# Scores in single precision on 32 by 64 tiles, values on 64-column tiles, a 64-row mask, the transposed context kept in memory, and new orders in both layers

## The reference, cut to what matters

```
x = x + tanh(g0) * attention0(norm(x), c)      # 16 heads of 8; mask in chunks of 32 keys
x = x + tanh(f0) * expert(norm(x))             # 8 experts 128->512->128, one for each token
x = x + tanh(g1) * attention1(norm(x), c)      # 16 heads of 8; causal mask and padding mask
x = x + tanh(f1) * mixture(norm(x))            # 16 experts: q, k, v of each token are sums over
                                               # experts, one head of 128, outputs again a sum
attention: softmax((xn Wq + bq)(c Wk + bk)^T / sqrt(8) + mask) (c Wv + bv) Wo + bo
```

## Time and profile before

| | |
|---|---|
| median of 3 runs | 1886.92 us (1884.77 to 1887.55) |
| profiled execution | 1886.17 us |
| its span | 1884.5 us, 51137 instructions |
| TensorE, matmul busy | 1728.3 us, 92% |
| VectorE / ScalarE / GpSimd busy | 1382.6 (73%) / 1132.2 (60%) / 1184.9 us (63%) |
| TensorE's granted clock over the span | 0.967 |
| first layer, experts, second layer | to about 428, 455 to 621, from there to the end |
| load of a slot, issue to landing | 2.1 us |

### The profile page before, as it was taken

The page is one execution under the profiler, slowest core; times in us unless marked ns, Lnnn a source line. Parts: engine busy times, 40 slices in busy tenths (PEclk is TensorE's granted clock), DMA queues, the critical chain, the costliest instruction groups (busy, mean ns, idle before and its releaser), DMA issues.

```text
span 1884.5 us, 51137 instructions
## 1 busy us (share of the span) xinstructions
PE 1728.3 (92%) x16279; PEld 1504.1 (80%) x16280; DVE 1382.6 (73%) x3767; ACT 1132.2 (60%) x2854; POOL 1184.9 (63%) x1682
## 2 busy tenths in 40 slices
PE   5999999983988589999999999999999999999986
PEld 4788888863888468888888888888888888888875
DVE  3676667654444247898888888898887888898875
ACT  3777777752544345666666666666666666666543
POOL 2444444444344347777877777787778777777764
PEclk8999999996999789999999999999999999999998
DMA  2311222233443100000000000000000000000000
GB/s 64 107 65 66 67 67 67 67 97 92 122 125 100 45 22 14 18 15 26 15 18 21 21 15 19 19 22 18 15 25 17 18 15 27 16 15 15 7 4 9
DMA packets 92898, 75.41 MB, mean 40 GB/s; under 512 B 13328, under 2 KB 80176, under 8 KB 92592
## 3 DMA queue, kind: packets, MB, share of 16 engines
q1 hardware_dynamic: 84992, 58.96, 10.4%
q0 software_dynamic: 5120, 12.62, 2.2%
q10 hardware_dynamic: 2608, 1.59, 0.4%
HBM read 36.91 MB, written 19.44 MB: 30 GB/s over the span
## 4 chain that ended last, share of the span: by engine, by line
PE 60%; DVE 7%; issue 5%; POOL 2%; SPq 1%; ACT 1%; DMA 1%; POOLq 0%; DVEq 0%; ACTq 0%
PE s_bank L1724 12%; PE s_bank L1726 10%; PE s_bank L1725 10%; PE po L1553 3%; PE tb L1538 3%; PE s_bank L1518 3%; PE s_bank L1666 2%; PE po L1678 2%; DVE qkv L1319 2%; PE s_bank L1855 2%; PE m L1803 1%; PE s_bank L1864 1%; DVE lg L1246 1%; PE tb L1724 1%; PE po L1724 1%
## 5 line engine op out<-in xcount | busy, mean ns | idle before, releaser
L694 POOL TENSOR_TENSOR qkv<-qkv,scaled 128x384 f32<-128x384 f32 x480 | 491.3, 1024 | 169.8 <-ACT scaled L907 130.7
L907 ACT ACTIVATE scaled<-s_bank,wg 128x384 f32<-128x384 f32 x448 | 252.9, 582 | 187.0 <-PE s_bank L1726 182.9
L1319 DVE SCALAR_TENSOR_TENSOR qkv<-s_bank,wg,qkv 128x384 f32<-128x384 f32 x448 | 274.6, 613 | 119.4 <-PE s_bank L1726 105.9
L1724 PE MATMUL s_bank<-proj_hi,hn_hi 128*128 128x384 f32 x896 | 340.0, 379 | 19.2 <-DVE qkv L1319 18.4
L1725 PE MATMUL s_bank<-proj_lo,hn_hi 128*128 128x384 f32 x896 | 302.7, 338 | 0.0
L1726 PE MATMUL s_bank<-proj_hi,hn_lo 128*128 128x384 f32 x896 | 302.4, 337 | 0.0
L793 ACT ACTIVATE pT<-tb 128x512 f32<-128x512 f32 x256 | 152.3, 595 | 75.9 <-PE tb L1538 75.4
L1724 PEld LDWEIGHTS s_bank<-proj_hi,hn_hi 128*128 128x128 f32 x896 | 169.6, 189 | 34.7 <-DVE qkv L1319 28.3
L1553 PEld LDWEIGHTS po<-vb,pT 128*64 128x64 f32 x4096 | 145.5, 137 | 62.3 <-issue 62.3
L1553 PE MATMUL po<-vb,pT 128*64 128x18 f32 x4096 | 170.9, 214 | 5.5 <-ACT pT L793 5.5
L1725 PEld LDWEIGHTS s_bank<-proj_lo,hn_hi 128*128 128x128 f32 x896 | 170.5, 190 | 0.8
(11 more groups left out here) (287 smaller groups left out, 4228.2 us busy)
## 6 DMA issues: line engine op xcount, KB each, us to landing
kx<-k SPq DMA_DIRECT2D x256, 64.0 KB
xs<-sorted_in SPq DMA_DIRECT2D x72, 128.5 KB, 2.1
cin<-in_ctx SPq DMA_DIRECT2D x64, 128.0 KB, 2.1
sorted_out<-yo SPq DMA_DIRECT2D x72, 64.0 KB, 1.8
xin<-in_x SPq DMA_DIRECT2D x32, 128.0 KB, 2.2
w<-in_L_ffn_W SPq DMA_DIRECT2D x16, 256.0 KB, 3.9
out_x<-res SPq DMA_DIRECT2D x32, 128.0 KB
sorted_in<-zrow ACTq DMA_DIRECT2D x1, 1156.5 KB, 6.5
```

Source lines behind the costliest of these rows:

```text
L694: g.tensor_tensor(into, into, scaled[m % SCALED][:, 0:cols], ALU.add).then_inc(dense_added, 1)
L907: ins = act.activation(into, bank[:, 0:3 * D], ACT.Copy, scale=wg[v % 4][:, 1, k:k + 1])
L1319: v.scalar_tensor_tensor(out=acc, in0=bank[:, 0:3 * D], scalar=wg[w % 4][:, 0, k:k + 1], in1=acc, op0=ALU.mult, op1=ALU.add).then_inc(dens ...
L1724: pe.matmul(bank[:, 0:cols], hi[:, tile], of(proj_hi), start=True, stop=False)
```

## The change

It has six parts. (a) Queries and keys are stored once, in full precision (`qT`, `kT`, `kx`), and the scores are 16 products on tiles of 32 rows by 64 columns; the corrections on VectorE are gone. (b) The masks follow: 8 products in both layers; in the second one half of the heads' mask stands on rows 0 to 63 and the other on 64 to 127. (c) Values are 8 products on 64-column tiles, a layout that puts even heads on partitions 0 to 63 and odd heads on 64 to 127. (d) The first layer's transposed context is stored to a buffer `ctx_cols` and loaded in the second, which transposes only the tokens. (e) The padding mask is loaded once as 128 by 64, transposed by TensorE and kept with keys on the partitions; its constants are built at body 0 of the first layer; the first norm is applied by GpSimd in the first layer (`apply_norm` there). (f) VectorE sums the outputs with small multiply-adds as they come, and all five engines have new orders.

The diff, cut to its core; allocations, semaphore names and waits that follow from these edits are left out.

```diff
 def place_keys(layer, v):
-        sp.dma_start(kx[r:P:4, r, :, :].bitcast(F32), k2[r:P:4, :, :].bitcast(F32)) ...
+        sp.dma_start(kx[r:P:4, r, :], kT[r:P:4, :]).then_inc(q["keys_placed"], 16)
+def store_context(v, par):
+    sp.wait_ge(s[0]["xcT_ready"], v + 1)
+    sp.dma_start(ctx_cols[bass.ds(v * P, P), :], xcT[par][:, 1, :]).then_inc(ctx_stored[par], 16)
 def body0(u, par):        # Sync
+        store_context(u + 2, par)
         place_keys(0, u + 2)
-            sp.wait_ge(setup["consts"], 5)
 def load_context(v):
-    sp.wait_ge(s[1]["xc_in_psum"], v - 1)
-    sp.dma_start(cin[par][:, :, :], tokens(a["ctx_1024"], v)) ...
+    sp.wait_ge(s[1]["qk_in_psum"], v - 1)
+    sp.wait_ge(s[1]["v_in_psum"], v - 1)
+    sp.dma_start(xcT[par][:, 1, :], ctx_cols[P * v:P * v + P, :]) ...
 def upper_consts():       # GpSimd, now called in body 0 of the first layer
-    g.tensor_copy(pad_u8[rows, :, :], pad_all[rows, :, h, :]) ...
 def pad_row(v):           # GpSimd: 3 steps on 128 columns become 2 on 256
+    step(g.tensor_tensor(pad_unit, bcast(not_causal, 4, 1), bcast(pad_keys[:, 4 * v:4 * v + 4], LEN, 2), ALU.mult))
+    g.tensor_tensor(mask_keys[v % 2], pad_unit, bcast(causal, 4, 1), ALU.add)
+def apply_norm(v, par):   # GpSimd, first layer, behind norm(0, v); ScalarE's is gone there
+        ins = g.tensor_scalar(xn[:, t, :], xin[par][:, t, :], rstd[:, t:t + 1], shift[:, 1, t:t + 1], ALU.mult, ALU.add)
 def body1(u):             # GpSimd
-    ... add(u, "q", 8, 9, 10); lower_heads(u - 1); add(u, "q", 11, 12, 13, 14, 15) ...
+    ... add(u, "q", 8, 9); lower_heads(u - 1); add(u, "q", 10); lower_hidden(u + 1); add(u, "q", 11, 12, 13, 14, 15) ...
 def keys(layer, v):       # ScalarE; queries(layer, v) is a second function like it
-    act.activation(k2[:, 0, :], m1[:, 256:512], ACT.Identity, bias=...)
+    act.activation(kT[:, :], m1[:, 256:512], ACT.Identity, bias=...).then_inc(q["k_ready"], 1)
-def lower_k(layer, w):    # VectorE, and lower_q
 def take_part(u, kind, k):   # VectorE, kind "o"
-    v.tensor_tensor(outs[:, 4 * k:4 * k + 4, :], bank, bcast(wg[w % 4][:, 0, 4 * k:4 * k + 4], D, 2), ALU.mult)
+    for e in range(4 * k, 4 * k + 4):
+        into, cols = halves[:, 0, e % 2, :], slice(D * (e % 4), D * (e % 4) + D)
+        if e < 2:
+            ins = v.tensor_scalar(into, bank[:, cols], wg[w % 4][:, 0, e:e + 1], None, ALU.mult)
+        else:
+            v.wait_ge(f["row_sums"], E1 * w + e - 1)
+            ins = v.scalar_tensor_tensor(out=into, in0=bank[:, cols], scalar=wg[w % 4][:, 0, e:e + 1],
+                                         in1=into, op0=ALU.mult, op1=ALU.add)
+        ins.then_inc(f["row_sums"], 1)
+    v.wait_ge(f["row_sums"], E1 * w + 4 * k + 4)
+    v.sem_inc(dense_used[0], 1)
-def fold, total_rows      # total_groups and total are half as wide
+def head_values(q, layer, par):   # TensorE, in values and upper_values
+    by_head = wv[layer][:, :].rearrange("c (r h d) -> c h r d", h=2, d=HD)
+    for seq in range(4):
+        for h in range(2):
+            ins = pe.matmul(m0[64 * h:64 * h + 64, LEN * seq:LEN * seq + LEN],
+                            xcT[par][:, 1, LEN * seq:LEN * seq + LEN], by_head[:, h, :, :], ...)
 def scores(layer, v, par):
-        pe.matmul(s_bank[j][:, :], early_rows[quad, :, :], late_keys[quad, :, :], ...)
+        for half in range(2):
+            pe.matmul(s_bank[j][64 * half:64 * half + 64, :], early_rows[quad, half, :], late_keys[quad, :, :], ...)
 def head_products(q, v):
-            for qs, ks in ((0, 0), (0, 1), (1, 0)):
-                for j in range(QUADS):
-                    ins = pe.matmul(s_bank[j][:, UNIT * t:UNIT * t + UNIT], beside[:, at:at + 2, :], kx[quad, :, ks, own], ...)
+            for j in range(QUADS):
+                quad = slice(32 * j, 32 * j + 32)
+                ins = pe.matmul(s_bank[j][64 * half:64 * half + 64, UNIT * t:UNIT * t + UNIT],
+                                qT[quad, own], kx[quad, :, own], ...)
 def upper_scores(u):
-    for j in range(QUADS):
-        pe.matmul(s_bank[j][:, :], identb[:, :], bcast(mask_pad[v % 2][:, :, :], 4, 2), ...)
+    for t in range(2):
+        mask = mask_keys[v % 2][:, 2 * t:2 * t + 2, :].rearrange("p h q -> p (h q)")
+        for j in (0, 2, 1, 3):
+            keys = slice(LEN * (j // 2), LEN * (j // 2) + LEN)
+            pe.matmul(s_bank[j][:, UNIT * t:UNIT * t + UNIT], mask[keys, :], bcast(identb[keys, keys], 4, 1), ...)
 def upper_in(v):
-    for t in range(2):
-        ins = pe.transpose(m0[:, P * (2 + t):P * (3 + t)], cin[v % 2][:, t, :], ident[:, :])
```

More of the change, by code:

```diff
@@ L233, in flamingo @@
             yo = [sb_first(f"yo{b}", [P, D]) for b in range(2)]
-        x3 = [sb(f"x3{b}", [P, 2, D]) for b in range(4)]
+        x3 = [sb(f"x3{b}", [P, 2, D]) for b in range(5)]
         hn = sb("hn", [P, 2, D])
@@ L530, in upper_consts @@
             def upper_consts():
-                for par in range(2):
-                    g.wait_ge(scattered[par], 16 * UNITS)
-                g.wait_ge(load["pad"], 16)
-                for h in range(2):
-                    rows = slice(LEN * h, LEN * h + LEN)
-                    g.tensor_copy(pad_u8[rows, :, :], pad_all[rows, :, h, :]).then_inc(setup["consts"], 1)
-                    g.wait_ge(setup["consts"], 4 + h)
-                for t, v in ((causal[:, :, :], 0.0), (not_causal[:, :, :], MASKED)):
+                for t, v in ((causal[:, :], 0.0), (not_causal[:, :], MASKED)):
                     done.free(g.memset(t, v))
@@ L1346, in total_groups @@
+                        v.wait_ge(f["row_sums"], E1 * w + 4 * k + 4)
+                        v.sem_inc(dense_used[0], 1)
             def total_groups(w):
                 if exists(w):
-                    step = Steps(v, f["sum_steps"], w, SUM)
-                    step.n = 3
                     v.wait_ge(dense_added, added_no(w + 1, "o", 3) + 1)
-                    step.wait()
-                    step.free(v.tensor_tensor(sums[:, :, 0:2, :], sums[:, :, 0:2, :], sums[:, :, 2:4, :], ALU.add))
+                    v.tensor_tensor(halves[:, 1, :, :], sums[:, 0:2, :], sums[:, 2:4, :], ALU.add)\
+                        .then_inc(f["sum_steps"], 1)
@@ L1354, in total @@
             def total(w):
                 if exists(w):
-                    step = Steps(v, f["sum_steps"], w, SUM)
-                    step.n = 4
-                    step.wait()
-                    step.free(v.tensor_tensor(oall[:, :, :], sums[:, :, 0, :], sums[:, :, 1, :], ALU.add))
-                    step.end()
+                    v.wait_ge(f["row_sums"], E1 * w + E1)
+                    v.wait_ge(f["sum_steps"], 2 * w + 1)
+                    v.tensor_tensor(oall[:, :, :], halves[:, :, 0, :], halves[:, :, 1, :], ALU.add)\
+                        .then_inc(f["sum_steps"], 1)
```

474 lines of the change are left out of this document (237 added, 237 removed).

## The result

The kernel after takes 1731.77 us (median of 4, 1726.85 to 1733.89), the kernel before 1887.24 beside it (4 runs): ratio 0.9174, 95% interval 0.915 to 0.920. The profiled execution has a span of 1732.2 us against 1884.5.

The account below looks back on a forecast made before the run. TensorE's list per unit was taken to bound both layers: 32 x 1.5 = 48, 32 x 0.95 = 30, and 9.5 between the layers make 88 us, so 1886 - 88 = 1798 us, range 1750 to 1860.

Parts of the forecast that it names:

- Part 1: Scores, both layers: 16 products on 32x64 tiles take 1.15 us instead of 1.63, 0.48 less per unit.
- rivals 1 and 4: Scores: rival 1 (0.10); or a product's second pass holds up all behind it, 1945 us, slower (0.06).
- rival 1: Column halves sharing row groups don't overlap: scores 1.8 us, values and masks without gain, 1858 us; chance 0.10.
- Part 2: Masks: 8 products on half tiles save 0.3 us per unit in the second layer, 0 in the first.
- Part 3: Values: 8 products 64 by 64 instead of 0.81 us, 0.3 less per unit in both layers.
- Part 4: Fewer changes of tile form at 0.2 us a trip: 0.6 less per second-layer unit, 0.4 in the first.
- Part 5: Context no longer transposed in the second layer: 0.2 us less per unit, later key transfers hidden.
- Part 6: Other engines: VectorE falls about 2.5 us of 32 per unit, its four small steps take 1.3 us; costed at 0.
- Part 7: Between first layer and experts: power function starts earlier, zero filling ends just before VectorE's part; 9.5 us less.
- The sum: Savings per unit 1.9 us (second layer) and 1.45 (first), credited 1.5 and 0.95; with 9.5 between layers, 88 us.
- Rival 3: Everything arrives and the 0.6 us of bank waits per unit goes as well: 1748 us; chance 0.12.
- Rival 2: Another bound comes up (VectorE's small steps, GpSimd, or a first-layer chain), layers give a third: 1850 us; chance 0.17.

Follow-up runs that it names:

- run 5: Kernel before with only VectorE's output sums changed, to sixteen multiply-adds of 128 columns: 1915.39 us, ratio 1.0158.
- run 3: Kernel before with only the scores changed, to 16 full-precision products on 32x64 tiles, no VectorE corrections: 1864.12 us, ratio 0.9897.
- run 7: Kernel after with the second layer's masks written four times: 1774.09 us, ratio 0.9408.
- run 6: Kernel after with 3.9 us of unused sums per unit on VectorE in the second layer: 1768.73 us, ratio 0.9396.
- Run 4: Kernel before with VectorE's output-sum steps one place later: with the short scores 1825.04 us, ratio 0.9691; without them 0.9952 and 0.9953.
- run 9: Kernel after with three more changes of tile form and back per second-layer unit: 1874.34 and 1869.68 us, kernel after beside the second 1827.1.

## Why the prediction was wrong, step by step

- **Part 1, scores.** Taken 1.15 us, measured 1.05 in the second layer and 0.98 in the first: rows and column halves do go side by side, rivals 1 and 4 are out. The Trainium skill's rule ("TensorE: Matmul & The Clock Gate", Part 3), that a weight load overlaps running products only when its row group differs, had led me to the 1.8 us of rival 1; the row of 1213.93 has 1.05, so in this kernel the rule does not decide.
- **Part 2, masks.** Taken 0.3 in the second layer, measured 0.43: the two halves of 64 rows go side by side nearly in full. In the first layer, taken 0, they came out shorter: with the start of the scores behind them 0.79 to 0.25, of which 0.27 was the wait for keys.
- **Part 3, values.** Taken 0.3, measured 0.29 in the second layer and 0.30 in the first.
- **Part 4, trips.** Taken 0.6, measured about 0.83 in the second layer (weighings 0.31, token scores 0.12, mixture passes 0.40).
- **Part 5, context.** 0.2 taken, 0.22 measured; the later keys are hidden, as said.
- **Part 6.** The small steps are 344 ns and a bank 1.35 us, near the 0.33 and 1.3 taken, and with the new order TensorE's waits for them are gone. Priced right, but only for the new order; in the old one they cost 31 us (run 5), which I had not seen. VectorE's busy time fell from 32.8 to 27.5 us in the units of the earlier trace rows and of the timeline above, 5.3 and not the 2.5 that I took.
- **Part 7, between the layers.** Taken 9.5, measured 6.2. The power function starts with its input as said; but the zero filling, which I placed just inside, ends last: it is issued 3.1 us behind the layer's end as before, and its largest part lands 9.6 us after its issue instead of 6.5. Timeline and a wait of SP's queue, kernel after:

```profile
395.81 2.93 POOL L645 TENSOR_TENSOR simn<-simq,half_pos 128x16 f32<-128x16 f32 x1 [4.39 <-DVE simq L1028]
...
405.06 5.83 SPq L460 DMA_DIRECT2D xs<-sorted_in  x6
...
408.63 2.05 PE L1675 MATMUL s_bank<-xsT,w_slot 128*128 128x128 f32 x8 [0.93 <-DVE xsT L1211]
```

```profile
SPq L456 <- DMA sorted_in<-zrow: 9.7, 1, 9.7
```

- **The sum.** This is the step that failed: "I credit 1.5 of 1.9 and 0.95 of 1.45", because "a wait now hidden behind TensorE's list shows once the list is shorter". The mechanism is real: in the second layer's old order it takes nearly all of it (run 3: 0.58 us saved, under 0.1 arrives) and not a fifth. But the new orders were part of the change, and in them nothing of it is left (run 7: one for one up to 35.4 us). I read the two orders only for trips, and gave them no value of their own. Start to start, the five items came to 2.35 instead of 1.9, and the bank wait, 0.84 us (0.6 in the earlier trace rows, which counts TensorE's idle time alone), came on top; the other rows nearly cancel: 3.1. Credited was 1.5: 1.6 x 32 = 51 of the 66 us missing. The rest is the first layer, 40.1 instead of 30, and the stretches around the steady units, less the transition.
- **Rival 3** (1748) had the mechanism, everything arrives and the bank wait goes, at 0.12; it is 16 us short, since its terms were the same. Its chance was the misjudgement: the wait stands in the earlier trace rows behind VectorE's accumulation, and the change did away with just those folds. **Rival 2** is excluded by the TensorE share of 99.8%; under ballast (run 6) it comes true.
- What would have shown it beforehand: following that 0.8 us wait back on VectorE to the 2 x 1.47 us of folds ahead of the unit's first parts, and asking where the new lists put that work. Run 4 bears this out when the scores are short; alone, the moved folds give 9 us. What stays open is how the gain of the new orders splits over TensorE, ScalarE and VectorE: no run has one of them in its old list and the others in the new one. For GpSimd there is one, and its order alone decides over 104 us.

## What to carry to other kernels

Where several engines run hand-written orders around one full list, a shorter list and the order are not two gains that add: test the wait behind each saving first (who ends it, what stands in front of that step on its engine). In this second layer the forms arrived in full where that wait was gone, and hardly at all where it was not; in the first layer, whose waits are others, the short scores alone brought 18 us in the old order. An engine that is 82% busy can set the unit by the place of one 5 us block, and a step that fits between alternating parts costs 31 us where two parts follow each other.

## What was not expected of the hardware

Sixteen single-precision products on 32x64 tiles (32 passes of 256 columns) take 1.05 us: 0.033 a pass, as fast as the old single-pass form on 32x128 tiles (48 in 1.63, 0.034), though a lone pass of this width would be 0.20 by the estimate from the earlier trace rows.

In two groups of runs the clock was another: the granted clock in the first layer (slices of 100 to 370) was 0.88 to 0.95 instead of 1.00, so its units took 12.8 us (after) and 13.6 (before with folds later) instead of 10.9 and 12.0. In the second layer the granted clock was 1.00, and yet the kernel after lost 1.6 us a unit. In its run there, VectorE's first maximum came 3.0 us after the first score, while the kernel after at the usual clock has 1.3 (1213.93 to 1215.24):

```profile
1258.52 1.12 PE L1524 MATMUL s_bank<-kx,qT 32*64 32x256 f32 x32
...
1261.48 1.89 DVE L1293 TENSOR_REDUCE mx<-s_bank 128x8 fp32r<-128x512 f32 x3 [2.95 <-remote]
...
1262.23 1.08 PE L1871 MATMUL s_bank<-mx,minus_ident 128*128 128x512 f32 x2 [1.12 <-DVE mx L1293]
```

With the trips parted (run 9) the median is 1.3 again, with the hidden rows early 2.1. TensorE's ends are modelled, so the products may have ended later than the row says; what delays them is open. The old form of the scores did not show it: 1.82 us in the runs with folds later at the lower clock, 1.83 in run 5 at the usual one. At the lower clock the change was worth 5.2% (0.9479), otherwise 8.3%.

The same VectorE step can take several times as long in another place of the order: the division of the token weights (`pbd`, 128x256) has a median of 1.89 us in the kernel before and 0.42 in the kernel after, and the unused sums of run 6 (128x512) take from 0.68 to 1.82 us each. What stretches them was not tested.
